# Pieces of weights two slots later, loads of 512 KB, and VectorE's slot with P's low half first

## What is computed

```python
q, k, v = heads(ln(x) @ w_q), heads(ln(x) @ w_k), heads(ln(x) @ w_v)    # 16 heads of 64
q, k = l2norm(q) * exp(scale), l2norm(k)
o = softmax(q @ k.T) @ v
x = x + ln(merge(o) @ w_out + b_out)
h = silu((x' @ w1.T) * s1) * ((x' @ w2.T) * s2)        # x' = ln(x); 256 -> 1024
h = gelu((h @ h1.T) * t1); h = gelu((h @ h2.T) * t2)   # 1024 -> 1024
x = x + ln((h @ w3.T) * s3)                            # 1024 -> 256
```

## Time and profile before

| | |
|---|---|
| time, median of 3 runs | 1980.66 us (1978.98 to 1986.99) |
| the profiled execution's own time | 1984.11 us |
| its span, first to last instruction | 1982.3 us |
| mean granted TensorE clock | 0.961 of full speed |
| TensorE busy (matmul / weight load) | 1753.8 / 1447.4 us |
| VectorE, ScalarE, GpSimd busy | 1222.7, 1011.9, 503.4 us |
| P (ScalarE, exp), first and last start | 46.6 to 1259.3 us |
| loads of pieces, first and last issue | 99.8 to 937.4 us |

### The profile page before, as it was taken

How to read it: one execution, slowest core, us unless ns; L and a number is a source line. 1 busy time by engine, 2 the same in 40 slices (tenths; PEclk the granted TensorE clock), 3 DMA queues, 4 the chain that set the end, 5 groups by cost and what they waited for, 6 DMA issues and landing times.

```text
span 1982.3 us, 24990 instructions
## 1 busy us (share of the span) xinstructions
PE 1753.8 (88%) x8576; PEld 1447.4 (73%) x8576; DVE 1222.7 (62%) x2125; ACT 1011.9 (51%) x1349; POOL 503.4 (25%) x590
## 2 busy tenths in 40 slices
PE   4899888989879888889889996689999999999997
PEld 3677667767767777667777875568778787787876
DVE  3687777687677787677677774544544545444453
ACT  2777666767657666656667764423232322313231
POOL 2334434344343444344333331000000000000000
PEclk8999999999999999999999998889999999999999
DMA  3445545545554654545444447220000000000000
GB/s 114 107 119 144 138 120 143 140 125 142 133 130 126 147 141 112 136 120 140 109 105 97 100 101 188 94 92 1 23 2 23 1 23 21 3 22 2 23 2 22
DMA packets 101061, 175.04 MB, mean 88 GB/s; under 512 B 27553, under 2 KB 48289, under 8 KB 99489
## 3 DMA queue, kind: packets, MB, share of 16 engines
q1 hardware_dynamic: 97872, 156.95, 31.4%
q10 hardware_dynamic: 1872, 11.67, 1.9%
q0 software_dynamic: 1152, 4.19, 0.5%
HBM read 56.91 MB, written 31.72 MB: 45 GB/s over the span
## 4 chain that ended last, share of the span: by engine, by line
PE 45%; DMA 18%; issue 14%; DVE 9%; POOL 7%; SPq 3%; ACT 2%; DVEq 0%; POOLq 0%; ACTq 0%
PE pair L1122 12%; PE pair L1123 12%; DMA work<-rows 11%; PE bank L1052 4%; PE bank L994 4%; PE bank L1066 3%; PE pair L1111 2%; POOL rs L401 2%; PE pair L1112 2%; DVE Pl L734 2%; DMA stg<-in_h 2%; DMA rows<-Rp 2%; DMA Dp<-work 2%; DVE work L750 2%; PE bank L1157 2%
## 5 line engine op out<-in xcount | busy, mean ns | idle before, releaser
L1052 PE MATMUL bank<-Ph,V 128*128 128x512 f32 x1024 | 383.0, 415 | 134.8 <-DVE Pl L734 90.9
L528 ACT ACTIVATE P<-pair,sh 128x1024 f32<-128x1024 f32 x256 | 286.4, 1119 | 277.3 <-DVE Pl L734 155.7
L1122 PE MATMUL pair<-hh,f 128*128 128x512 f32 x1024 | 403.6, 394 | 16.3 <-issue 9.2
L1123 PE MATMUL pair<-hl,f 128*128 128x512 f32 x1024 | 402.2, 393 | 0.0
L1052 PEld LDWEIGHTS bank<-Ph,V 128*128 128x128 f32 x1024 | 199.8, 195 | 214.3 <-issue 165.7
L734 DVE TENSOR_TENSOR Pl<-P,Ph 128x1024 fp32r<-128x1024 f32 x256 | 314.6, 1229 | 1.4 <-ACT Ph L533 0.4
L568 ACT ACTIVATE hr<-pair,ct 128x512 f32<-128x512 f32 x128 | 88.3, 690 | 375.9 <-PE pair L1123 375.9
L533 ACT ACTIVATE Ph<-P 128x1024 fp32r<-128x1024 f32 x256 | 271.6, 1061 | 8.1
L1122 PEld LDWEIGHTS pair<-hh,f 128*128 128x128 f32 x1024 | 194.4, 190 | 62.5 <-issue 13.5
L1123 PEld LDWEIGHTS pair<-hl,f 128*128 128x128 f32 x1024 | 194.5, 190 | 40.5
L401 POOL TENSOR_TENSOR rs<-ss,half 128x8 f32<-128x8 f32 x128 | 213.6, 1669 | 10.7
(11 more groups left out here) (100 smaller groups left out, 2896.4 us busy)
## 6 DMA issues: line engine op xcount, KB each, us to landing
stack<-turned SPq DMA_DIRECT2D x128, 384.0 KB, 4.4
stack<-turned SPq DMA_DIRECT2D x128, 256.0 KB, 4.8
work<-rows SPq DMA_DIRECT2D x64, 256.0 KB
high<-sth SPq DMA_DIRECT2D x44, 256.0 KB, 2.5
low<-stg SPq DMA_DIRECT2D x44, 256.0 KB, 2.3
f<-high ACTq DMA_DIRECT2D x11, 1024.0 KB, 5.0
stg<-in_h SPq DMA_DIRECT2D x32, 256.0 KB, 6.9
xt<-in_x SPq DMA_DIRECT2D x8, 512.0 KB, 7.6
```

Of the source, the lines that this page charges most:

```text
L528: e.activation(M.P[:, i % 2, :], M.SB[i % 2][:, :], ACT.Exp, bias=M.sh[:, h:h + 1]).then_inc(S["exp"])
L1052: d = e.matmul(M.OB[:, :], v, p[:, u % 3, j * 512:(j + 1) * 512], start=jt == 0 and m == 0, stop=jt == 3 and m == 2)
L1122: e.matmul(ps, f[:, k, ms], M.hh[src][:, k, :], start=k == 0, stop=False)
L1123: d = e.matmul(ps, f[:, k, ms], M.hl[src][:, k, :], start=False, stop=k == KH - 1 and not low)
```

## The change

Three things are done at once.

1. The steps of a piece fall two slots later: piece n has its load in slot 14 + 4n instead of 12 + 4n, and the other steps in the three slots behind it.
2. `load_f` issues each megabyte as two parts of 512 KB, one part per slot over twice the slots (22 issues for 11). To make room, the load of x1 for the feed-forward part (`load_xv`, which now waits for `free0` alone), its layer norm and its turn are moved three or four slots up, in all five programs and in the bank plan.
3. VectorE's slot is put in another order: `o_low`, `invert`, layer norms, `count_piece`, `normal`, `head_scale` of the slot before, then `p_low` of the *same* slot i, then `head_sums`, `v_low`, `turn_low`, `add_part`, `x_low` and the rest. The instructions are the same.

The core of the diff (the moves of feed-forward steps in the programs of SyncE, GpSimd, VectorE and TensorE are alike, and left out but for the first):

```diff
@@ bank_plan
-        if i == NU:
+        if i == NU - 3:
             order += [(("x3", 0), i), (("x3", 1), i)]
...
-LOADS = {0: 2, 1: 4, 2: 4, 3: 1}
+LOADS = {0: 4, 1: 8, 2: 8, 3: 2}
...
 def piece_at(i, step):
-    n, r = divmod(i - 12, 4)
+    n, r = divmod(i - 14, 4)
     return n if r == step and 0 <= n < PIECES else None
@@ sync_program
-        free1(q)
+        free0(q)
         e.dma_start(M.xv[:, b % 2, :, :], M.x1[b]).then_inc(S[f"x1{b % 2}"], 16)
...
-        if i == NU - 7:
+        if i == NU - 11:
             load_xv(0)
@@ act_program
-        if i in (NU - 10, NU - 9):
+        if NU - 10 <= i < NU - 6:
             load_f(0, i - NU + 10)
-        if NU - 8 <= i < NU - 4:
-            load_f(1, i - NU + 8)
-        if NU + 3 <= i < NU + 7:
+        if NU - 6 <= i < NU + 2:
+            load_f(1, i - NU + 6)
+        if NU + 3 <= i < NU + 11:
             load_f(2, i - NU - 3)
-        if i == NU + 9:
-            load_f(3, 0)
-        if i == NU:
+        if i in (NU + 11, NU + 12):
+            load_f(3, i - NU - 11)
+        if i == NU - 3:
             x3_high(0)
@@ vector_program
     for i in range(SLOTS):
-        if 0 <= i - 1 < NU:
-            p_low(i - 1)
...
+        if piece_at(i, 2) is not None:
+            count_piece(piece_at(i, 2))
+        if i % 4 == 1 and 0 <= n - 3 < NP:
+            normal(n - 3)
+        for u in tiles_of(i - 1) if i else []:
+            head_scale(u)
+        if live:
+            p_low(i)
+        for u in tiles_of(i):
+            head_sums(u)
+        if values_of(i) is not None:
+            v_low(values_of(i))
+        if pair_of(i) is not None:
+            turn_low(pair_of(i), 1)
+            turn_low(pair_of(i), 0)
...
-        if i in (NU - 5, NU - 4):
-            norm3(0, 2 * (i - NU + 5))
...
+        if i in (NU - 9, NU - 8):
+            norm3(0, 2 * (i - NU + 9))
@@ build
-        M.loads = [[(M.f1[:, :, :], M.hi12[:, 0:2, :]), (M.f2[:, :, :], M.hi12[:, 2:4, :])]]
-        M.loads += [[(f[:, k:k + 2, :], high[:, k:k + 2, :]) for k in range(0, KH, 2)]
-                    for f, high in ((M.f3, M.hi3), (M.f4, M.hi4))]
-        M.loads.append([(M.f5[:, :, :], M.hi5)])
+        M.loads = [[(f[:, k, :], M.hi12[:, 2 * j + k, :]) for j, f in enumerate((M.f1, M.f2)) for k in range(2)]]
+        M.loads += [[(f[:, k, :], high[:, k, :]) for k in range(KH)] for f, high in ((M.f3, M.hi3), (M.f4, M.hi4))]
+        M.loads.append([(M.f5[:, k:k + 4, :], M.hi5[:, k:k + 4, :]) for k in (0, 4)])
```

More of the change, by code:

```diff
@@ L459, in pool_program @@
             flag(layer_of(n))
-        if i == NU - 3:
+        if i == NU - 7:
             norm_root3(0)
@@ L895, in vector_program @@
             invert(n - 2)
[L896 to L915, removed]
         if 0 <= pb < B - 1:
@@ L926, in vector_program @@
                 ln1b(b + 1, i32_ - 16)
-            if i32_ in (20, 21):
-                x_low(b + 1, i32_ - 20)
+        if piece_at(i, 2) is not None:
[13 more added lines that the diff above has]
+            turn_low(pair_of(i), 0)
+        if quad_of(i) is not None:
+            add_part(quad_of(i), 0)
+            add_part(quad_of(i), 1)
+        if b + 1 < B and i32_ in (20, 21):
+            x_low(b + 1, i32_ - 20)
+        if tail == 8:
+            for t in range(NT):
+                finish(B - 1, t)
+        if tail == 9:
+            for t in range(NT):
+                finish2(B - 1, t)
         if HEAD <= i < HEAD + 7:
@@ L932, in vector_program @@
                 halves(0, 0, m)
-        if piece_at(i, 2) is not None:
-            count_piece(piece_at(i, 2))
-        if i in (NU - 5, NU - 4):
-            norm3(0, 2 * (i - NU + 5))
[L937 to L941, removed]
+        if i in (NU - 9, NU - 8):
+            norm3(0, 2 * (i - NU + 9))
+            norm3(0, 2 * (i - NU + 9) + 1)
+        if i in (NU - 6, NU - 5):
+            norm3b(0, 2 * (i - NU + 6))
+            norm3b(0, 2 * (i - NU + 6) + 1)
+        if i == NU - 3:
             x3_low(0)
```

## The result

The changed kernel takes **2134.05 us** (median of four, 2132.73 to 2137.5) against 1979.82 for the kernel before; the ratio is 1.0774, 95% interval 1.0745 to 1.0803. So it is 154 us slower; the forecast was 2033, at most 2085.

What follows compares the result with a forecast made beforehand. TensorE was taken as the busiest engine, starved by waits, with a ring of the weight pieces setting the pace after the edit. 1984.1 +74 +6 -5 -23 = 2036, less 3.4 for the median: 2033 us, range 1965 to 2085.

Steps and rivals of the forecast that it cites:

- Part 1: VectorE's order in attention: earlier `p_low` alone gives 30 us less, but not where pieces are loaded.
- Part 2: Steps of a piece two slots later: the piece stage goes from 837.6 to 912 us, +74 (+9 to +119).
- The turns' ring: Piece stage: load, landing, split, count, `p_low`, `turn_low`, stacks, next load set the pace, 42.4 us per eight slots.
- the landing: Piece stage: a load takes 6.1 us from issue to its cast, twice per eight slots.
- Rival (a): Piece stage: loads land near 3.6 us, the ring doesn't bind, TensorE and VectorE's order set the pace; 1889 us, chance 0.12.
- The signs: Piece stage: loads 20 to 22 us apart, `count_piece` waiting over 200 us, TensorE idle behind it, SP waiting for turns.
- Part 3: GpSimd's waits behind the four flags, three of which move from slot 11 to 13 modulo 32: +6 us.
- Part 4: Attention between the last piece and the passage: half of the remaining excess is order alone, -5 us (0 to -10).
- Part 5: Passage to feed-forward: half the bytes per slot shorten the chain of `normal`, -23 us (-12 to -32).
- The first link: Passage, up to the first `normal`: earlier sums and a spread of 10 us instead of 21.3, -17 us.
- Rival (d): Passage: two 512 KB parts in flight hold the spread as one of 1 MB does, gain 0; 2056 us, chance 0.12.
- Rival (c): Piece stage: idle TensorE gets a lower clock, 1 to 3 us more per round; 2054 to 2098 us, chance 0.15.

Runs made afterwards that it cites:

- `p_low` alone: Kernel before with `p_low(i)` in its own slot ahead of the sums, instead of at the head of the next slot: 1927.7 us, ratio 0.9747.
- the ladder: Kernel before with `p_low` in its own slot, 1928 us; `normal` behind it, both ahead of the sums, 2066; `normal` ahead of `p_low`, 2125; VectorE's whole new order, 2160.
- the order alone: Kernel before with VectorE's new order of the attention slots and nothing else changed: 2160.4 us, ratio 1.0925.
- the kernel with the passage's moves alone: Kernel before with 512 KB load parts and x's load, norm and turn earlier; pieces and VectorE's slots as before: 1976.95 us, ratio 1.0016.
- the one with two moves: Kernel before with `p_low` in its own slot, then `normal`, both ahead of the sums and `turn_low`: 2065.7 us; with SyncE's stacks behind the row sums 2066.2.

## Why the prediction was right and wrong

**What bounds it.** "TensorE is the busiest engine" and its 104 us of waits were read right. I then took the pieces for what made eight slots 39 us instead of 33, and never added up the reciprocals' loop, though the earlier trace rows (7.25 us for a spread) and the earlier trace rows had its links. In before it takes 35.3 past the pieces, and `normal` waits 0.1 to 0.4 us on average: so the loop is just closed, with hardly any slack.

**Part 1.** Its first half was right and too small: `p_low` alone gives 47 to 51 us where I said 30, and 35 of it in the piece stage (812.2 for 846.8), where I had left it out because of part 2's ring. The step that failed is the sentence that "what `normal` loses to late reciprocals is cushioned by some 2.5 us more". `normal` stood in the sum at 1.4 us, its busy time. Its wait is not its own: whatever stands behind it is late by it, and comes back as a later `invert`. That is the bulk of the result: +138 and +60 of the ladder, and 129 of the 154 us when `normal` alone is put back.

**Part 2.** 912 us of piece stage forecast, 918 with the flags, 932 measured: that was luck. The turns' ring doesn't bind. The kernel after with `normal` behind `turn_low` and `head_scale` behind `p_low` still has all of that ring but `normal`'s 1.4 us: by the prediction's terms 41.0 per eight slots or 881 us from first to last load, and it took 849.3 (964.0 less 114.7), the flags' waits included. The term that was too long is the landing: a load lands in 3.0 us in that kernel (3.3 in after) and not in 6.1, which takes some 6 us off the 42.4, to an estimated 36. Rival (a) had just this ("a load that no longer shares its queue with the spread could come near" 3.6), at 0.12; it then took VectorE's new order for free. The low store behind stacks I had put at 4.6; it took 5.1. The signs told the two apart at once: `count_piece` at 59 us and not over 200, and +42 us where no piece runs.

**Part 3.** +6 (0 to 12); alone 28 to 33. A wait of 7.7 us was in the earlier trace rows, but I priced it by what it covers and not by where it ends: one slot ahead of a head root, with TensorE's next tile behind it.

**Part 4.** -5, measured +42, and +37 with the order alone: the same failed step as in part 1, and the plainest disproof.

**Part 5.** -23, measured -1 in after and nothing alone. The first link did shorten: in the kernel with the passage's moves alone the spread issued at 1217.77 reached `normal` at 1233.67, 15.9 us for 21.3; I had said 10. Then the next took longer (20.9 us from `normal` to `normal` for 16.1), so that the last stood at 1290.06 for 1291.50:

```profile
1233.67 1.40 DVE L750 TENSOR_TENSOR work<-work 64x512 f32<-64x512 f32 x2 [12.29 <-DMA work<-rows]
...
1254.61 1.40 DVE L750 TENSOR_TENSOR work<-work 64x512 f32<-64x512 f32 x2 [10.16 <-DMA work<-rows]
...
1271.96 1.41 DVE L750 TENSOR_TENSOR work<-work 64x512 f32<-64x512 f32 x2 [4.36 <-issue]
...
1290.06 1.41 DVE L750 TENSOR_TENSOR work<-work 64x512 f32<-64x512 f32 x2 [6.95 <-DMA work<-rows]
```

Rival (d), that two halves in flight hold the spread as one whole does, is what this looks like. The halves landed in 4.5 us each for 5.0 of the whole: some 100 us of landing in all for 55. The matmuls that read them stood idle no longer for it (11.5 us without a releaser shown up to 1500 us, as in the kernel before). The 1 MiB that the Trainium skill (DMA: Bandwidth & Descriptors, Rules for kernel authors) wants bore neither way: the same bytes in halves left the time at 1.0016. The fit that the prediction took from the same page of the Trainium skill stands there for transfers that GpSimd issues, and these were issued by ScalarE; no term of the sum rested on it.

**Rival (c)**, the clock, I had hung on the pieces' ring. It came with the other one: TensorE's busy time rose by 51 us at equal work. How much of that a kernel with the ring could have had back is not shown, since a waiting TensorE may take it at no cost.

**Open** is why the pieces' two slots and the passage's moves, +28 and 0 alone, take 26 us off in the presence of the order (2160 to 2134), and why SyncE's stacks behind the sums gave back 41 us in the kernel after and none in the one with two moves. Past the pieces, `normal` to `invert` fell by 3.0 us per eight slots there and 1.9 came back in the other column; in the one with two moves it was 2.4 and 2.0.

## To carry to other kernels

An instruction that waits for a transfer belongs at the end of its in-order slot: before moving it forward, list what stands behind it and ask whether one of those feeds the same transfer the next time round, also by way of another engine that takes its work in order (here GpSimd's `head_root` ahead of `o_high`); if so, the order adds to a loop, and its length (here 42 us in place of 34) is the pace, however idle the engine is. Add up every loop that crosses a transfer, also those that the edit doesn't name, and test a candidate on a stretch where it alone runs. A stage time that comes out as forecast proves no mechanism; the signs named for it do.

## What the runs showed of the hardware

- A reduction over partitions on GpSimd took 0.40 us in itself in the kernel after, with 5.6 to 6.1 us of idle engine before it and 6.9 to 7.1 before the head root's first instruction behind it (L398); with the pieces two slots later alone the second wait was 7.5 to 10.6. The trace has sixteen MODIFY_POOL_CONFIG on GpSimd's queue for the four reductions, two at the start of each of the two idle stretches. With the reduction left out there are none but the two at the program's start, and 2.6 to 3.0 us of idle time before the head root. The Trainium skill (GPSIMD Engine Reference, Terminology) says of that instruction that it fetches a loadable code library at run time, which would fit; the waits are shown as idle time without a releaser, and no run here takes the library apart from the reduction.
- A 256 KB load of a piece landed in 6.9 us (median) where its issue fell on the slot of the reciprocals' spread, and in 3.0 to 3.4 two slots later; the 256 KB low store went the other way, 2.3 to 3.0 and then 5.0 to 5.2 (6.3 in the kernel after with the stacks moved). The twelve kernels with the old places had 6.9 to 7.6 for the load, the seven with the new ones 3.0 to 3.4, whatever VectorE's order.
- Issuing the small store of the reciprocals took SyncE 0.32 us with a quiet queue and 1.81 behind four stacks; the stacks of that stretch 0.5 to 0.7 for the first two and 1.1 to 1.6 for the next two.
- Behind TensorE's stall of 10.5 us at the flag (pieces two slots later), the granted clock was 0.50 for 2.9 us, that is 1.2 GHz, and a matmul of L994 took 0.63 us (the first 0.79); from 289.65 on, at 2.4 GHz, one took 0.39 to 0.40. The busy view of the two stretches (columns as in the earlier trace rows):

```profile
282.10:285.00 2.90, 2.87 (x7) 2.19 (x8) 2.30 (x3) 0.00 (x0) 1.18 (x1) 0.50 0.01 3
287.00:291.00 4.00, 4.00 (x16) 3.23 (x15) 3.02 (x6) 2.91 (x4) 1.69 (x2) 0.85 0.45 91
```
